# Decoder layer on one core: attention's last chunk loads the next stage's first chunk, and the fallback's code moves into that stage's block

## What is computed

```
x = layernorm(x + attn(x))        # qkv = x @ w_qkv.T; softmax(q k^T / sqrt(32)) v; @ w_out.T + b_out
x = layernorm(x + xattn(x, ctx))  # softmax(x ctx^T / sqrt(32)) ctx @ W_out.T
x = layernorm(x + ffn(x))         # quantised: silu(x @ w_gate.T) * (x @ w_up.T), then @ w_down.T
```

## Time and profile before

| | |
|---|---|
| runs of the kernel before | 1917.68 us median (1915.24 to 1918.08, 3 runs) |
| the profiled execution's own time | 1916.18 us |
| its span | 1914.4 us |
| TensorE busy | 1795.4 us, 94% |
| VectorE busy | 1462.4 us, 76% |
| ScalarE busy | 1452.3 us, 76% |
| GpSimd busy | 161.4 us, 8% |
| mean granted TensorE clock | 0.965 of full |

### The profile page before, as it was taken

The page is one execution under the profiler, slowest core; times in us unless marked ns, Lnnn a source line. Parts: engine busy times, 40 slices in busy tenths (PEclk is TensorE's granted clock), DMA queues, the critical chain, the costliest instruction groups (busy, mean ns, idle before and its releaser), DMA issues. The chain is left out here.

```text
span 1914.4 us, 40608 instructions
## 1 busy us (share of the span) xinstructions
PE 1795.4 (94%) x16002; PEld 895.6 (47%) x16028; DVE 1462.4 (76%) x1579; ACT 1452.3 (76%) x1572; POOL 161.4 (8%) x131
## 2 busy tenths in 40 slices
PE   8999997999999999999999999999849995999686
PEld 6777773333333333333333333333327773444332
DVE  5444445989898998989898998989816776688687
ACT  5343345999999999999999999999715553565475
POOL 0000000000000000000000000000022220000164
PEclk9999998999999999999999999999969995899898
DMA  8655655536446364464464373554654320142274
GB/s 294 221 205 195 223 203 185 108 82 169 97 105 161 85 149 111 105 161 89 100 166 100 89 175 80 133 131 91 154 190 165 133 88 1 61 181 121 97 270 170
DMA packets 111645, 270.07 MB, mean 141 GB/s; under 512 B 7956, under 2 KB 26516, under 8 KB 101780
## 3 DMA queue, kind: packets, MB, share of 16 engines
q1 hardware_dynamic: 98324, 193.05, 27.8%
q0 software_dynamic: 9216, 67.11, 18.9%
q10 hardware_dynamic: 3968, 7.86, 1.1%
HBM read 115.95 MB, written 84.93 MB: 105 GB/s over the span
## 5 line engine op out<-in xcount | busy, mean ns | idle before, releaser
L793 DVE TENSOR_TENSOR dve_sum<-dve_sum,probs 128x2048 f32<-128x2048 f32 x320 | 733.0, 2291 | 9.8
L713 ACT ACTIVATE probs<-score_others,shift_now 128x1536 f32<-128x1536 f32 x384 | 598.0, 1557 | 0.0
L845 PE MATMUL score_first<-q_parts,k_parts 32*128 32x512 f32 x1536 | 492.9, 426 | 10.1 <-DMA v_group<-v_scratch 9.1
L845 PE MATMUL score_others<-q_parts,k_parts 32*128 32x512 f32 x4608 | 497.5, 426 | 0.0
L845 PEld LDWEIGHTS score_first<-q_parts,k_parts 32*128 32x128 f32 x1536 | 244.3, 183 | 374.6 <-ACT probs L712 184.5
L875 PE MATMUL mixed_ps<-probs,v_group 128*32 128x512 f32 (+1 forms) x3840 | 407.9, 515 | 1.1 <-ACT probs L713 0.2
L712 ACT ACTIVATE probs<-score_first,shift_now 128x512 f32<-128x512 f32 x384 | 267.0, 695 | 11.3 <-PE score_others L845 8.3
L845 PEld LDWEIGHTS score_others<-q_parts,k_parts 32*128 32x128 f32 x4608 | 251.7, 184 | 3.8
L713 ACT ACTIVATE probs_paired<-score_others,shift_now 128x1536 f32<-128x1536 f32 x128 | 198.3, 1550 | 0.0
L875 PEld LDWEIGHTS mixed_ps<-probs,v_group 128*32 128x32 f32 x3840 | 93.0, 108 | 161.5 <-issue 115.4
L875 PE MATMUL mixed_ps<-probs_paired,v_group 128*32 128x256 f32 (+1 forms) x1792 | 142.7, 416 | 0.0
(11 more groups left out here) (206 smaller groups left out, 2206.0 us busy)
## 6 DMA issues: line engine op xcount, KB each, us to landing
probs_paired<-probs_paired POOLq DMA_DIRECT2D x64, 1024.0 KB, 8.0
k_parts<-k_scratch SPq DMA_DIRECT2D x36, 512.0 KB, 7.1
q_parts<-q_scratch SPq DMA_DIRECT2D x33, 512.0 KB, 6.5
o_scratch<-out_parts SPq DMA_DIRECT2D x33, 512.0 KB, 2.8
h_scratch<-h SPq DMA_DIRECT2D x6, 2816.0 KB, 8.1
h<-h_scratch SPq DMA_DIRECT2D x6, 2816.0 KB, 10.4
k_scratch<-parts SPq DMA_DIRECT2D x32, 512.0 KB, 3.2
q_scratch<-parts SPq DMA_DIRECT2D x32, 512.0 KB, 2.7
```

The costliest lines, as they stand in the source:

```text
L713: nc.scalar.activation(block_probs(k)[:, CH:HPG * CH], score_others[n % 2][:], ACT.Exp, bias=shift[:, c:c + 1], scale=SCALE).then_inc(prob ...
L793: nc.vector.tensor_tensor(total[:], first[:], block_probs(k)[:], ALU.add).then_inc(dve_added, 1)
L845: last = nc.tensor.matmul(out, k_parts[rows, a, k * P:(k + 1) * P], q_parts[f % 2][rows, b, :], start=t == 0, stop=t == len(TERMS) - 1)
```

## The change

- Keys, values, `w_out`'s parts and the first query buffer are allocated for attention and `mix` together. `mix` takes the four key pieces as its first `o_in`, the four value pieces as its tokens and the first query buffer as a part of its second `o_in`.
- SyncE's loop runs 7 iterations. The eighth is written out, loads no keys and values, and loads `mix`'s first chunk: each piece of `o` when the last scores on that key piece are made, each tile of tokens when the last values on that value piece are used. SyncE waits for the store of the last result in `mix`, ahead of the load of its second chunk. The bias is loaded at attention's start.
- `finish` is split. Behind the loop VectorE makes the extremes between `invert` and `divide`.
- `true_max` and `attend_exact` no longer have blocks. They return functions that `mix`'s block calls, under one branch on each engine. TensorE tests for 0, has the whole stage in that case, and behind it, in the other case, the fallback and the stage a second time.
- GpSimd adds the first chunk's bias before its memsets, and clears the semaphores behind them. Tokens are loaded and biased in four tiles where it was one load and two halves.

The diff, without the re-indented bodies of the fallback:

```diff
+def load_first_o(sp, scr, keep, k):
+    src = scr.o[:, k * P:(k + 1) * P, 0:CH].rearrange("s p t -> p s t")
+    sp.dma_start(keep.keys[k][:].bitcast(F32), src).then_inc(keep.o_here, 16)
+
+def load_first_tokens(sp, io, keep, t):
+    sp.dma_start(keep.values[t][:].rearrange("p k c -> p (k c)"), io.x[t * P:(t + 1) * P, :]).then_inc(keep.tokens_here, 16)
...
-                with sp.Fori(0, ITERS) as it:
+                sp.dma_start(keep.bias[:], io.b_out.partition_broadcast(P)).then_inc(keep.bias_in, 16)
+                with sp.Fori(0, ITERS - 1) as it:
...
+                last = ITERS - 1
+                for c in range(CPB):
+                    sp.wait_ge(scores_done, 1 + last * BLOCKS + c * KB)
+                    if c < CPB - 1:
+                        load_q(last // BATCH, last % BATCH, c + 1)
+                    store(last, c)
+
+                sp.wait_ge(stored, 1 + 16 * (last * CPB + 1))
+                for piece in range(PIECES):
+                    sp.wait_ge(scores_done, 1 + ITERS * BLOCKS - (PIECES - 1 - piece) * KPP)
+                    load_first_o(sp, scr, keep, piece)
+                for piece in range(PIECES):
+                    sp.wait_ge(mixed_done, (ITERS + 1) * BLOCKS - (PIECES - 1 - piece) * KPP)
+                    load_first_tokens(sp, io, keep, piece)
                 store(ITERS, 0)
-                sp.wait_ge(stored, 1 + 16 * (ITERS * CPB + 1))
...
-                finish(ITERS, 0)
-
+                invert(ITERS * CPB)
                 v.wait_ge(extremes_done, 2 + 2 * (ITERS * CPB + 1))
...
+                divide(ITERS * CPB)
                 v.wait_ge(row_done, 1)
...
-                load_mix(0, 0)
-                sp.dma_start(bias[:], io.b_out.partition_broadcast(P)).then_inc(bias_in, 16)
-                load_tokens(0)
+                    for t in range(T):
+                        sp.dma_start(tokens[t], x_src[:, bass.ds(chunk, 1), t].rearrange("p o d -> p (o d)")).then_inc(x_here, 16)
+
+                with only_if(sp, keep):
...
                 sp.dma_start(xw, io.xw_out_t.rearrange("(k p) e -> p k e", p=P)).then_inc(xw_in, 16)
+                sp.wait_ge(keep.stored, O_STORED)
                 load_mix(CPB, 1)
...
-                pool.sem_clear(keep.spent)
...
+                    for t in range(T):
+                        nc.gpsimd.tensor_tensor(tokens[t], tokens[t], keep.bias[:], ALU.add).then_inc(biased, 1)
+
+                with only_if(pool, keep):
...
                 nc.gpsimd.memset(eps[:], EPS).then_inc(eps_done, 1)
+                pool.wait_ge(keep.bias_in, 16)
+                add_bias(None)
...
+                with pe.If(pe.value_load(keep.wide[0:1, 0:1], min_val=0, max_val=1) == 0):
+                    whole()
+                with pe.Else():
+                    keep.true_max.tensor(pe)
+                    pe.wait_ge(keep.max_over, 1)
+                    keep.attend_exact.tensor(pe)
+                    pe.wait_ge(keep.again_over, 1)
+                    whole()
```

More of the change, by code:

```diff
@@ L943, in attend_exact @@
         k_stack = sb("k_stack", [STACK, HPG, SEQ], F32R)
-        q_stack = [sb(f"q_stack{u}", [STACK, HPG, CH], F32R) for u in range(2)]
-        v_group = sb("v_group", [P, KB, P], F32)
+        q_stack = [keep.keys[2 * u:2 * u + 2] for u in range(2)]
+        v_group = keep.values
         probs = [sb(f"probs{i}", [P, HPG * CH], F32) for i in range(P_SLOTS)]
@@ L950, in attend_exact @@
         normal = [sb(f"normal{u}", [P, CH], F32) for u in range(2)]
-        out_parts = [sb(f"out_parts{u}", [P, 2, CH], F32R) for u in range(2)]
+        out_parts = [keep.q_first, sb("out_second", [P, 2, CH], F32R)]
         scores = [ps(f"scores{i}", [P, 2 * CH], F32) for i in range(S_SLOTS)]
@@ L1514, in project @@
                 def project(n, u, loads, tiles, first=False):
-                    pe.wait_ge(o_here[u], 16 * KT * loads)
+                    if first:
+                        pe.wait_ge(keep.o_here, 16 * KT)
+                    else:
+                        pe.wait_ge(o_here[u], 16 * KT * loads)
                     for t in tiles:
@@ L2067, in decoder @@
         project(nc, io, scr, keep)
-        keep.w_parts = sb("w_out_parts", [P, 2, KT, D], F32R)
+        keep.q_first = far("first_queries", [P, 2, CH], F32R)
+        keep.keys = [far("key_piece0", [P, 2, PIECE * P], F32R)]
+        keep.values = [far("value_piece0", [P, PIECE, P], F32)]
+        keep.keys += [far(f"key_piece{i}", [P, 2, PIECE * P], F32R) for i in range(1, KB // PIECE)]
+        keep.values += [far(f"value_piece{i}", [P, PIECE, P], F32) for i in range(1, KB // PIECE)]
+        keep.w_parts = far("w_out_parts", [P, 2, KT, D], F32R)
+        keep.bias = far("out_bias", [P, D], F32)
         attend(nc, io, scr, keep)
-        true_max(nc, scr, keep)
-        attend_exact(nc, scr, keep)
+        keep.true_max, keep.attend_exact = true_max(nc, scr, keep), attend_exact(nc, scr, keep)
         keep.x2 = sb("x2", [P, TOK // P, D], F32)
```

633 lines of the change are left out of this document (328 added, 305 removed).

## The result

| | before | changed |
|---|---|---|
| first comparison, medians | 1916.56 us (4 runs) | 1896.90 us (4 runs, 1896.27 to 1898.96) |
| ratio, 95% interval | | 0.990 (0.9886 to 0.9914) |
| second comparison, medians | 1918.21 us (17 runs) | 1896.90 us (4 runs, 1894.76 to 1898.90) |
| ratio, 95% interval | | 0.989 (0.9874 to 0.9906) |

The kernel is 20 to 21 us faster, and the forecast of 1895.0 us is 1.9 us off, within its range. The first profiled execution of the changed kernel took 1898.96 us, the longest of its four; its span is 1896.8 us, its mean granted clock 0.969 (before 1914.4 and 0.965). A second profile of both kernels was taken too.

A forecast was written before the change was run, and what follows sets the result against it. The handover from attention to `mix` was taken as the gap where nothing computes. Terms -0.7 -1.4 -10.0 -11.5 +1.3 -0.6 = -22.9 turn 1916.18 into 1893.3 us, with 1.5 to the median 1894.8, said as 1895; range 1890 to 1900.

The forecast's parts named there:

- Loads of the last iteration: Attention's last iteration: without key and value loads queued before it, the second accumulating join lands earlier, -0.7 us.
- rival 1: Attention's end: the first loads share with the second join and slow it, +1.7 instead of -0.7, 1897.2 us; chance 0.10.
- End of attention: Attention's end: extremes beside the division, and no wait for the last store in the block, release earlier, -1.4 us.
- Two blocks removed: Between attention and `mix`: both fallback blocks' jumps and barriers go, 1392.8 to 1402.82, -10.0 us.
- First loads out of the gap: Start of `mix`: the time from its first loads to its first matmul, 1402.82 to 1414.28, goes, -11.5 us.
- What the new block adds: TensorE at `mix`'s entry: one read of `wide`, a branch not taken and two semaphore increments, +1.3 us.
- Rival 2: TensorE's entry to `mix`: it reaches its stage only by a jump, paying 3.4 or 4.1 us, 1898.6 us; chance 0.06.
- Inside the projection: First projection of `mix`: the third tile's wait for biased tokens goes, -0.6 us.
- Clock: First projection of `mix`: the low clock, 0.50 for its first 4.6 us, is kept as a cost unchanged.
- Rival 3: First projection: the clock stays high through the shorter pause, 4.6 us of matmuls take half, 1892.5 us; chance 0.10.
- Hidden edits: `mix`'s loop and end: four token loads, the moved bias load and TensorE's closing jump fit into existing slack, no term.
- The sum: Whole kernel: the six terms together give -22.9 us.

The follow-up runs named there:

- experiment 3: Changed kernel, but SyncE loads the first attention output and tokens at the head of the mixing block, not inside attention: 1908.06 us, ratio 0.9953.
- experiment 8: Changed kernel, but each pass of the mixing loop issues the attention output's four loads ahead of the tokens' four: 1900.88 us, ratio 0.9904.
- experiment 6: Changed kernel, but with division ahead of the extremes and SyncE waiting for the last store inside attention's block, as before: 1898.48 us, ratio 0.989.
- experiment 5: Changed kernel, but TensorE tests for the fallback first and reaches the mixing stage by a taken branch: 1899.41 us, ratio 0.9899.
- experiments 3 to 9: Seven variants of the changed kernel, each undoing or reordering a part of it: medians from 1896.97 to 1908.06 us.
- experiment 12: Changed kernel, but the first projection's tile 0 runs between attention's sums and extremes, tile 1 ahead of TensorE's read in mixing: 1894.40 us, ratio 0.9876.
- experiment 4: Changed kernel, but maxima and exact attention sit again in two skipped blocks of their own; first loads stay in attention: 1906.01 us, ratio 0.9936.
- experiment 10: Changed kernel, but TensorE runs the first projection's first two tiles ahead of its read of `wide` and its branch: 1895.82 us, ratio 0.9887.

## Why the prediction was right, point by point

*Loads of the last iteration (-0.7).* The join came early enough, as assumed: 8.1 us for 9.7, and no wait for it. But the reasons given for it were incomplete. The bounds took 0.75 MB as issued behind the join in the kernel before; its queue has two pieces of keys and two of values there (1373.80 to 1379.24), 1.5 MB, as much as in the changed kernel. So it isn't the amount that made 9.7 us into 8.1; what did is open. The first loads do slow the join, by 1.2 us (experiment 3), as rival 1 said; the sums were already held by VectorE's copy (1.61 us), so it cost nothing. And both profiles of before had the clock at 0.50 during the sums, which the prediction did not count; experiment 8 has the same dip by itself and prices it at 1.2 us. With 9.85 + 1.40 (experiment 6) + 1.2, 0.3 to 0.9 us of before's tail of 12.74 and 13.35 are left for the join, whose waits there were 0.21 and 0.97 us. Whether the dip belongs to the kernel before or to luck is open: two of two executions of it had it, and one of the twelve of the changed kernel and its variants.

*End of attention (-1.4).* 1.40 in the tail, by the two mechanisms named: some 1.1 us from the new order (1.0 was said) and 0.3 from the wait for the store, which, and not `wide`, had set the release. The end of the block behind the write of `wide` took 0.52 us, for the half microsecond assumed.

*Two blocks removed (-10.0).* 9.95 and 10.56 in the two profiles of before, 11.20 when put back.

*First loads out of the gap (-11.5).* +11.2 in the median, +11.6 in the cut, when undone, though by another sum: read and jump ahead of the loads, quicker loads, and 0.5 us of clock in the projection.

*What the new block adds (+1.3).* The term that was mis-sized: 1.93. I took the read of `wide` from before, where the 1.0 us to the branch includes a read of 0.49. Without SyncE's wait for the store, the release and the read come sooner behind store and write, and the read itself takes 1.02: 0.5 of the 0.6 us that were missing. Rival 2 stayed what it was, a price of 3.6 to 4.1 us (experiment 5) that the code avoids.

*Inside the projection (-0.6).* 13.31 us from the first matmul to the turn instead of 13.70: -0.4, and 13.06 for 13.91 in the second profiles. No wait for tokens. But most of these differences are clock. In ten executions (the second of before, both of the changed kernel, experiments 3 to 9) this stretch takes 10.9 us plus half of the time that the clock stood at 0.50 in it, which was 3.5 to 6.0 us; all ten agree with that within 0.1 us. Only the first profile of before has 11.35 in place of 10.9: it had the 0.6 us wait, the second had none. The term stood for a loss that one of two executions had.

*Clock.* Kept, as assumed: 0.50 for the first 4.8 and 4.3 us of the projection in the two profiles. Rival 3 did not happen; the pause is 4.5 us now, and the clock had already fallen at the extremes. By the Trainium skill (TensorE: Matmul & The Clock Gate, "What's actually happening") activity releases the throttle; experiment 12 agrees, 0.50 for 3.4 us once a tile of work stands in the pause.

*Hidden edits.* VectorE's jump (1392.60 to 1395.65) was hidden behind the first tile, which VectorE added at 1398.30. TensorE's closing jump ended 7 us ahead of the barrier. Token loads in four pieces cost 0.8 and 1.4 us of the cover for the tokens issued at 1431.66 and 1452.75 and 0.4 or less later, about the 1 us assumed, and no wait. SyncE's context and weight loads began at 1395.65, took 1.5 us for the 5.3 counted and held nobody. The loop's 0.25 us a double pass and the 0.2 in the rest, +0.7 in all, was in no term; its cause is open (experiment 4 has 41.5 us a double pass, half of it gone).

*The sum.* -22.9 was forecast. Attention's start to `mix`'s end lost 22.3 by the means of two profiles each, and the whole 19.7 in the first comparison and 21.3 in the second. That the stages come within 0.6 us of the sum is partly luck: the tail gave 3.2 us for the 2.1 of its two terms, by the low clock in both profiles of before, and this made up for the read of `wide`, the wait in the projection that was not there the second time, and the loop. Of the 1.6 to 3.2 us missing in the whole, what lies outside these stages does not point at the change: the parts before and behind scatter by as much from one execution to the next (projections 304.8 to 308.7, the last stage 115.7 to 118.9).

## What to carry to other kernels

Where a stage begins with loads whose inputs have long been there, count what lies between the last useful instruction and the first of the next stage, and move the loads over the boundary into buffers that fall free; here that gave 11 us once. A rarely taken fallback is cheapest behind the code of the engine that others wait for, with its jump at the end, and in the same block as the stage, so that no barrier of its own is paid: here 10 to 11 us for the blocks, of which 3.6 to 4.1 would be lost again with TensorE's branch the other way round. When a wait is removed ahead of a barrier, look at what the next instruction then runs into, and when the bound moves (here to VectorE's jump), give the idle engine work from behind the barrier.

## What the runs showed of the hardware

- A read of one word (`wide`) into the sequencers takes 0.49 us on TensorE where it starts 1.9 us or more behind the issue of the last store and 1.1 us or more behind the word's write, and 1.01 to 1.03 us where it starts within 1.2 and 0.9 us. In experiment 10 both lengths stand in one execution: 1.04 to 1.06 us for the engines that read at once, 0.49 for TensorE 2.8 us later. Which of the two, store or write, makes it long was not separated. A second read of the same word by TensorE, in the second skipped block of the kernel before, took 0.31 us.
- A taken jump over the same code differs from build to build and from execution to execution: 3.4, 3.7, 3.8 us for TensorE's first, 4.1, 4.4, 4.4 for its second. One jump over both bodies (experiment 5) took 4.2 us, no more than the second alone. VectorE's is recorded with 0.06 us, and its next instruction stands 3.0 us behind (1392.60 to 1395.65).
- An accumulating join of 1 MB took 6.9 us without the first loads beside it, 8.1 with them, 9.7 beside keys and values, with 1.5 MB issued behind it in both cases.
- The first projection, 48 matmuls, took 10.9 us plus half of the time that the clock stood at 0.50 in it (3.5 to 6.0 us in ten executions). So the moment at which the clock comes back moved this stretch between 12.7 and 13.9 us with nothing changed in it.
